# The end of an attention in a four-layer transformer kernel: transposes on TensorE against a rearranging transfer and three VectorE steps

## The chip, the cores and the metric

One core of one Trainium2 chip runs the whole program in one launch. The metric is the device time of an execution in microseconds (us), lower is better; the time before is the median of three executions, and one more execution was profiled. Engine names are those of the profile: PE (TensorE), PEld (TensorE's weight load), DVE (VectorE), ACT (ScalarE), POOL (GpSimd), SP (SyncE, which here only issues transfers).

## What is computed

Sixteen sequences of 256 tokens with 256 features pass four layers. There are seven attentions for each sequence (numbered 0 to 6; 0, 2 and 4 are self-attentions, 0 and 2 causal, 4 with a mask; 1, 3, 5 and 6 attend to a context of 77 tokens), two feed-forward blocks and one mixture of 8 experts. Every attention has 16 heads of 16 features:

```
q = q_in @ wq + bq;  k = kv_in @ wk + bk;  v = kv_in @ wv + bv
p = softmax(q @ k.T / sqrt(16))            # per head
o = concat_heads(p @ v)                    # tokens x 256
x = x + o @ wo + bo                        # then a layer norm
```

With a softmax whose rows sum to one, adding bv to v and adding it to o is the same, and the kernel adds it to o.

## The kernel before

The program has three phases. Phase a takes each sequence through attentions 0 to 3 and the first feed-forward block and routes its tokens to experts; phase b runs the experts, 39 groups of 256 tokens; phase c does attentions 4 to 6 and the second feed-forward block. In a and c a sequence is a lane: several sequences are under way at once (LANES: 6 in a, 7 in c), each at another place of its chain, so that one's transfers and small steps lie under another's matrix work.

The order on each engine is written out ahead by a planner (`Plan.run`). Each piece of work is a step with an engine, an assumed duration `us`, for transfers an assumed landing time `lag` (times a factor, 1.35), the steps it comes `after`, and the buffers that it takes and gives back. The planner places steps greedily, the earliest start first, and among equals by urgency; a table `AHEAD` shifts the urgency of each kind of step at each attention. What comes out is a fixed order for each engine: an engine that waits for one step waits with everything behind it. The names of the kinds are the ones used below:

- `proj`, `high`, `rest`, `middle`, `low`, `copy`: queries and keys are projected (PE, L684), cut into three bf16 parts by ACT, DVE and POOL, and stacked by SP's transfers (L1347) into `qs` and `ks`.
- `qm`, `max`: scores with queries on partitions (PE, L706, with the mask matmuls L839 and L843), and their maxima (DVE, L1085), one PSUM bank at a time, of eight.
- `shift_high` to `shift_low`, `turn_shift`, `turned_shift`, `shift_in`: the maxima go as three bf16 parts (DVE, L1091 to L1104) through a transpose (PE, L714) and ACT into `qs` by a transfer (L1350).
- `km`, `exp`: scores with keys on partitions (PE, L726), and their exponentials (ACT, L936) into `prob`.
- `pv`: values times probabilities (PE, L742), with 32 stationary columns for each head: 16 values, a column of ones for the sum, and 15 columns that belong to the next head and aren't used.
- the end: `raw` (ACT, L947) copies a bank of 128 partitions (4 heads of 32 rows) by 512 columns (2 groups of heads, 256 tokens) from PSUM; `turn_raw` (PE, L752) makes 4 transposes for each half of the tokens, 8 in all; `recip` and `weigh` (DVE, L1110 and L1116) divide each half by its 16 sums, with tokens on partitions; `turn_normed` (PE, L761) transposes back, 4 of them; `heads` (ACT, L953) adds bv as a per-partition bias while copying from PSUM.
- `out`, `add`: the output projection (PE, L778) and the addition to x (DVE, L1122). L778 is also the second matrix of the feed-forward blocks and experts, L794 the first.
- norms: `stats`, `moments`, `apply` (DVE, L1053, L1060, L1067) with two small POOL steps between them, then `turn` (PE, L675).
- phase c gets its tokens by `enter` and four `gather`s for each sequence (POOL, L1303) into `pair_y`.

In the names of tiles `a_`, `b_` and `c_` stand for the phase.

## Time and profile before

| | |
|---|---|
| median of three executions | 3278.52 us |
| lowest and highest | 3277.52 and 3300.14 us |
| the profiled execution, its own time | 3263.0 us |
| its span, first to last instruction | 3261.2 us |
| mean granted clock of TensorE | 0.960 of full |
| attentions | 112 (16 sequences x 7): 64 in phase a, 48 in c |

The span leaves 1.8 us around it. The profiled execution was 15.5 us (0.5%) under the median, so a sum made in the trace is put on the median's scale by the factor 3278.52 / 3263.0 = 1.0048.

### The profile page before, as it was taken

To read this page: it belongs to the slowest core of one execution; us is meant where nothing else is said; L and a number is where in the kernel's file an instruction comes from. 1 tells how busy PE (TensorE), PEld (TensorE's weight loads), DVE (VectorE), ACT (ScalarE), POOL (GpSimd) and SP (SyncE) were. 2 spreads that over 40 slices of the span, in tenths; PEclk is the share of its full clock that TensorE was granted. 3 is DMA by queue.
4 is the path that set the end of the run, shared out by engine and by line. 5 is a ranking of instruction groups with operands and counts; after the bars stand their busy time and mean duration, and the time that the engine had idled before them with its cause. 6 is when DMAs were issued, how large, how long until landed. Compare 5 with 4: busy or idle time off the path is not lost. (4 is left out here: it accounts for less than half of the span.)

```text
span 3261.2 us, 61820 instructions
## 1 busy us (share of the span) xinstructions
PE 3031.6 (93%) x23913; PEld 2467.9 (76%) x24016; DVE 1574.7 (48%) x4057; ACT 1548.4 (47%) x3403; POOL 871.0 (27%) x991
## 2 busy tenths in 40 slices
PE   7899999999999999885999999889999999999996
PEld 5788877788887788663888888656777777777774
DVE  4544556655466656353101011166555666666552
ACT  4555555564655656352222222145556555665552
POOL 3112224232223423222000000152233343433241
PEclk8999999899999999995999999989999999999997
DMA  9635446535445743832666666374425564556231
GB/s 169 95 54 67 63 54 99 81 65 70 78 59 73 108 59 70 186 49 96 235 220 222 198 204 202 101 118 64 60 49 75 77 85 62 78 76 78 39 57 26
DMA packets 394607, 319.34 MB, mean 98 GB/s; under 512 B 151711, under 2 KB 378271, under 8 KB 394303
## 3 DMA queue, kind: packets, MB, share of 16 engines
q1 hardware_dynamic: 371062, 276.77, 47.1%
q0 software_dynamic: 8272, 23.73, 3.1%
q10 hardware_dynamic: 14981, 14.89, 1.6%
q8 instruction: 190, 3.11, 0.5%
q14 instruction: 102, 0.84, 0.1%
HBM read 134.33 MB, written 37.22 MB: 53 GB/s over the span
## 5 line engine op out<-in xcount | busy, mean ns | idle before, releaser
L1085 DVE TENSOR_REDUCE a_maxima<-a_bank 128x2 f32<-128x512 f32 (+3 forms) x576 | 340.1, 646 | 136.8 <-PE a_bank L706 136.2
L936 ACT ACTIVATE a_prob<-a_bank 128x512 f32<-128x512 f32 (+1 forms) x640 | 338.1, 599 | 121.3 <-PE a_bank L726 114.9
L936 ACT ACTIVATE c_prob<-c_bank 128x512 f32<-128x512 f32 (+1 forms) x512 | 263.7, 599 | 142.5 <-PE c_bank L726 140.8
L972 ACT ACTIVATE b_group_hidden<-b_bank,b_b 128x256 f32<-128x256 f32 x312 | 131.0, 471 | 421.3 <-PE b_bank L794 421.3
L1085 DVE TENSOR_REDUCE c_maxima<-c_bank 128x2 f32<-128x512 f32 (+2 forms) x448 | 266.3, 638 | 93.1 <-PE c_bank L706 91.8
L839 PE MATMUL a_bank<-a_causal_b,keep_identb 128*128 128x256 bf16 (+1 forms) x768 | 246.2, 321 | 43.0 <-DMA a_qs<-a_shift 25.5
L794 PE MATMUL b_bank<-b_group_xt,b_w 128*128 128x256 f32 x1248 | 284.0, 381 | 0.8 <-DVE b_group_xt L1126 0.8
L778 PE MATMUL b_bank<-b_w,b_group_hidden 128*128 128x256 f32 x1248 | 275.8, 379 | 0.9 <-ACT b_group_hidden L972 0.9
L778 PEld LDWEIGHTS b_bank<-b_w,b_group_hidden 128*128 128x128 f32 x1248 | 237.0, 190 | 33.5 <-ACT b_group_hidden L972 1.3
L794 PEld LDWEIGHTS b_bank<-b_group_xt,b_w 128*128 128x128 f32 x1248 | 235.5, 191 | 31.9 <-DVE b_group_xt L1126 1.2
L1131 DVE TENSOR_TENSOR b_group_y<-b_bank,b_b 128x512 f32<-128x512 f32 x39 | 27.0, 691 | 364.4 <-PE b_bank L778 364.4
L1122 DVE TENSOR_TENSOR a_tok<-a_bank,a_tok 128x512 f32<-128x512 f32 x80 | 55.2, 690 | 190.5 <-PE a_bank L778 190.2
L706 PE MATMUL a_bank<-a_ks,a_qs 96*128 96x128 bf16 x1536 | 145.4, 223 | 0.0
L726 PE MATMUL a_bank<-a_qs,a_ks 99*128 99x128 bf16 x1536 | 145.0, 223 | 0.0
L706 PEld LDWEIGHTS a_bank<-a_ks,a_qs 96*128 96x128 bf16 x1536 | 122.9, 100 | 25.0 <-issue 3.3
L726 PEld LDWEIGHTS a_bank<-a_qs,a_ks 99*128 99x128 bf16 x1536 | 122.7, 100 | 22.5 <-issue 1.4
L778 PE MATMUL a_bank<-a_at_o,a_heads 128*128 128x256 f32 x512 | 132.0, 403 | 6.3 <-ACT a_heads L953 6.0
L684 PE MATMUL a_bank<-a_xt,a_at_q 128*128 128x256 f32 x512 | 126.7, 391 | 5.0 <-ACT a_xt L909 2.9
L1284 POOL TENSOR_TENSOR c_tok<-c_tok,weights_row_L_xattn_ln_g 128x512 f32<-128x512 f32 x64 | 81.4, 1273 | 185.6 <-PE c_bank L675 185.6
L1292 POOL TENSOR_TENSOR a_parts_q<-a_rest,a_parts_q 128x512 bf16<-128x512 f32 x64 | 74.2, 1159 | 206.6 <-ACT a_parts_q L925 206.5
L947 ACT ACTIVATE a_raw<-a_bank 128x512 f32<-128x512 f32 x128 | 76.5, 598 | 108.1 <-PE a_bank L742 107.9
L794 PE MATMUL c_bank<-c_xt,c_weights_f 128*128 128x256 f32 x512 | 122.4, 383 | 0.8 <-ACT c_xt L909 0.7
(239 smaller groups left out, 6496.2 us busy)
## 6 DMA issues: line engine op xcount, KB each, us to landing
b_w<-in_L_xattn_e_w SPq DMA_DIRECT2D x78, 1024.0 KB, 7.1
a_qs<-a_parts_q SPq DMA_DIRECT2D x384, 128.0 KB, 4.4
c_qs<-c_parts_q SPq DMA_DIRECT2D x288, 128.0 KB, 4.3
a_ks<-a_parts_k SPq DMA_DIRECT2D x192, 128.0 KB
c_ks<-c_parts_k SPq DMA_DIRECT2D x96, 128.0 KB
b_group_x<-sorted_in SPq DMA_DIRECT2D x39, 256.0 KB, 6.6
sorted_out<-b_group_y ACTq DMA_DIRECT2D x39, 256.0 KB, 4.8
sorted_in<-a_zeros SPq DMA_DIRECT2D x8, 1024.0 KB, 10.4
```

Source lines behind the costliest of these rows:

```text
L684: ins = pe.matmul(bank[:, 0, m * n:(m + 1) * n], weight[:, kt, m * P:(m + 1) * P], xt[:, kt, 0:n], start=(kt == 0), stop=(kt == KT - 1))
L706: ins = pe.matmul(bank[:, 0, to:to + m], qs[0:STACK, h, q * P:(q + 1) * P], ks[0:STACK, h, kt * P:kt * P + m], start=(at in CROSS), stop=( ...
L726: ins = pe.matmul(bank[0:kn, 0, to:to + m], ks[0:STACK + NPART, h, kt * P:kt * P + kn], qs[0:STACK + NPART, h, q0:q0 + m], start=(at in CR ...
L778: ins = pe.matmul(bank[:, 0, q * D:(q + 1) * D], heads[:, kt, q * P:(q + 1) * P], weight[:, kt, :], start=(kt == 0), stop=(kt == kts - 1))
L794: ins = pe.matmul(bank[:, 0, j * S:(j + 1) * S], weight[:, kt, f * P:(f + 1) * P], xt[:, kt, :], start=(kt == 0), stop=(kt == KT - 1))
L839: pe.matmul(blocks, k.identb, k.causal[:, keys_first, :].unsqueeze(1).broadcast_to([P, 4 // step, P]), start=True, stop=False)
L936: act.activation(prob[0:rows, first:first + cols], bank[0:rows, 0, 0:cols], ACT.Exp, scale=SCALE).then_inc(k.own(s), 1)
L947: act.activation(tile(s, "raw"), tile(s, "bank")[:, 0, :], ACT.Copy).then_inc(k.own(s), 1)
L972: ins = act.activation(hidden[:, f, :], bank[:, 0, j * S:(j + 1) * S], ACT.Gelu, bias=b1[:, f:f + 1])
L1085: v.tensor_reduce(maxima[:, q:q + qn, h:h + n].rearrange("p q h -> p h q"), bank[:, 0, 0:cols].rearrange("p (j q n) -> p j q n", j=n, q=qn ...
L1284: pool.tensor_tensor(x, x, over(k.gains[at][0]), ALU.mult).then_inc(k.own(s), 1)
L1292: pool.tensor_tensor(parts[:, 2, :, 0:n], rest[:, :, 0:n], parts[:, 1, :, 0:n], ALU.subtract).then_inc(k.own(s), 1)
```

## The change

It replaces the end of every attention.

- The values are interleaved with ones: the stationary block of a head is now 16 pairs (value, 1), so row 2d of a head's 32 rows is the output of feature d, and row 2d + 1 the sum. `pv` has the same shapes.
- `align` and `align_last`, two SP transfers for each attention, take `raw` (128 partitions x 512) to `aligned`, 64 partitions each: even rows to slot 0 and odd rows to slot 1 of the destination partition. Values and their sums then lie beside each other, with features on partitions and tokens along the row.
- DVE takes the reciprocal of the sums (128 x 512 elements), multiplies (128 x 512), and adds bv (two instructions of 128 x 256), all in place in SBUF. The output projection reads `aligned` slot 0. The rows of wo and bv are permuted ahead on the host's side of the inputs to fit.
- `turn_raw`, `turn_normed` and ACT's `heads` are gone, and their buffers with them.
- Buffers: `tok` 7 to 8, `loaded` 2 to 1 and `prob` 4 to 3 in phase a; `raw` 4 to 3; `aligned` 2 new; `pair_y` 2 to 1 in phase c. Small tiles share an allocation.
- LANES is 7 in phase a. The planner's AHEAD tables, its rate for each phase, its landing factor in phase a, and its price of a gather are other numbers.
- The load of ones at the start of phase c goes on ACT's queue. The context weights of attention 1 are a load of their own ("1c"), ahead of its q and o weights.

```
-LANES = {"a": 6, "c": 7}
+LANES = {"a": 7, "c": 7}
...
             plan.step("scalar", "raw", b, at, i, us=0.65, after=[("pv", b, at, i)], gives=["bank"], bank=pv, raw=raw)
-    raws = {f"raw{i}": ("raw", (i,) + lab) for i in range(2)}
-    normed, heads = ("normed", lab), ("heads", lab)
-    for q in range(QT):
-        bank, recip = ("bank", ("turn_raw", q) + lab), ("recip", (q,) + lab)
-        plan.step("tensor", "turn_raw", b, at, q, us=0.44, after=[("raw", b, at, 0), ("raw", b, at, 1)]
...
-        plan.step("vector", "recip", b, at, q, us=0.28, after=[("turn_raw", b, at, q)], bank=bank, recip=recip)
-        plan.step("vector", "weigh", b, at, q, us=0.45, after=[("recip", b, at, q)] + ([("weigh", b, at, 0)] if q else []),
...
-    plan.step("tensor", "turn_normed", b, at, us=0.44, after=[("weigh", b, at, 0), ("weigh", b, at, 1)], takes=["bank", "heads"],
...
-    plan.step("scalar", "heads", b, at, us=0.87, after=[("turn_normed", b, at)], gives=["bank"],
...
+            plan.step("sync", "align_last" if i else "align", b, at, us=0.65, lag=3.5, after=[("raw", b, at, i)], behind=[("align", b, at)] if i else [],
+                      gives=["raw"], landing="aligned", raw=raw, aligned=aligned)
+    plan.step("vector", "recip", b, at, us=0.6, after=[("align", b, at), ("align_last", b, at)], aligned=aligned)
+    plan.step("vector", "weigh", b, at, us=0.6, after=[("recip", b, at)], aligned=aligned)
+    plan.step("vector", "heads", b, at, us=0.6, after=[("weigh", b, at)], aligned=aligned)
+    return aligned
...
-               "projs": 0.8, ("projs", 0): -0.4, ("projs", 1): -0.2, "pvs": -1.0, ("pvs", 0): -0.1, "scores": 0.1,
+               ("projs", 0): -0.4, ("projs", 1): -1.8, ("projs", 3): -0.4, ("projs", "l0_ff"): -0.6, "pvs": -1.0,
...
-    plan.step("sync", "load", -1, "c", "ones", us=2.0, lag=2.0, takes=["w"], landing="w", transfers=len(loads["c", "ones"]),
+    plan.step("scalar", "load", -1, "c", "ones", us=2.0, lag=2.0, takes=["w"], landing="w", transfers=len(loads["c", "ones"]),
...
-        plan.step("gpsimd", "gather", b, "c", j, us=0.95, lag=4.0, behind=[("gather", b, "c", j - 1)] if j else [("enter", b, "c")],
+        plan.step("gpsimd", "gather", b, "c", j, us=1.25, lag=4.0, behind=[("gather", b, "c", j - 1)] if j else [("enter", b, "c")],
...
-                                        values[0:kn, kt, (4 * g + j) * (HD + 1):(4 * g + j) * (HD + 1) + 32],
+                                        values[0:kn, kt, 4 * g + j, :, :].rearrange("p d k -> p (d k)"),
...
         elif s.kind == "recip":
...
-            v.reciprocal(tile(s, "recip"), per_head[:, :, HD]).then_inc(k.own(s), 1)
+            sums = tile(s, "aligned")[:, 1]
+            until.wait_ge(*done("align", b, at))
+            until.wait_ge(*done("align_last", b, at))
+            v.reciprocal(sums, sums).then_inc(k.own(s), 1)
         elif s.kind == "weigh":
...
+            v.tensor_tensor(aligned[:, 0], aligned[:, 0], aligned[:, 1], ALU.mult).then_inc(k.own(s), 1)
+        elif s.kind == "heads":
+            heads, bias = tile(s, "aligned")[:, 0], k.biases[at][2]
+            until.wait_ge(*done("weigh", b, at))
+            for kt in range(KT):
+                ins = v.tensor_scalar(heads[:, kt, :], heads[:, kt, :], bias[:, kt:kt + 1], None, ALU.add)
+            ins.then_inc(k.own(s), 1)
...
+        elif s.kind in ("align", "align_last"):
+            i, half = int(s.kind == "align_last"), P // 2
+            until.wait_ge(*done("raw", b, at, i))
+            if i == 0:
+                until.wait_ge(*freed(s, "aligned"))
+            sp.dma_start(tile(s, "aligned")[i * half:(i + 1) * half], tile(s, "raw")).then_inc(k.own(s), 16)
...
-    pool("tok", 7 if name == "a" else 8, [P, QT, D])
-    pool("loaded", 2, [P, QT, D])
+    pool("tok", 8, [P, QT, D])
+    pool("loaded", 1 if name == "a" else 2, [P, QT, D])
...
-    pool("values", 2, [P, QT, H + 1, HD + 1])
+    pool("values", 2, [P, QT, H, HD, 2])
...
-    pool("prob", 4 if name == "a" else 3, [P, prob_width])
-    pool("raw", 4, [P, 2 * S])
-    pool("normed", 1, [P, QT, D])
-    pool("recip", 4, [P, H])
-    pool("heads", 1, [P, KT, S])
+    pool("prob", 3, [P, prob_width])
+    pool("raw", 3, [P, 2 * S])
+    pool("aligned", 2, [P, 2, KT, S])
...
-        plan.run("a", 20.0, ahead_of("a"), 1.35)
+        plan.run("a", 20.0, ahead_of("a"), 1.2)
...
-        lane_pool("pair_y", 2, [P, 2 * QT, D])
+        lane_pool("pair_y", 1, [P, 2 * QT, D])
...
-        plan.run("c", 28.0, ahead_of("c"), 1.35)
+        plan.run("c", 32.2, ahead_of("c"), 1.35)
```

The planner's new numbers move nearly every row, so the order is shown at two places. First DVE in the middle of phase c of the kernel before, in a run of maxima (L1085): the end of an attention is the four rows L1110 and L1116, one pair for each half of the tokens.

```order
L1075 SCALAR_TENSOR_TENSOR c_rest<-c_bank,keep_columns,c_parts_k 128x77 x2
L1085 TENSOR_REDUCE c_maxima<-c_bank 128x2
L1110 RECIPROCAL c_recip<-c_bank 128x16
L1116 TENSOR_TENSOR c_normed<-c_bank,c_recip 128x256
L1110 RECIPROCAL c_recip<-c_bank 128x16
L1116 TENSOR_TENSOR c_normed<-c_bank,c_recip 128x256
L1085 TENSOR_REDUCE c_maxima<-c_bank 128x2 x5
L1122 TENSOR_TENSOR c_tok<-c_bank,c_tok 128x512
```

The same engine and phase in the changed kernel, in which the line numbers are others (L1058 are the maxima, L1083 the reciprocal, L1087 `weigh`, L1092 `heads`, L1048 `rest`, L1064 to L1077 the four `shift` steps). This is sequence 8, attention 4.

```order
L1083 RECIPROCAL c_aligned<-c_aligned 128x512
L1058 TENSOR_REDUCE c_maxima<-c_bank 128x2
L1087 TENSOR_TENSOR c_aligned<-c_aligned 128x512
L1058 TENSOR_REDUCE c_maxima<-c_bank 128x3x2 x2
L1048 SCALAR_TENSOR_TENSOR c_rest<-c_bank,keep_columns,c_parts_k 128x77 x2
L1058 TENSOR_REDUCE c_maxima<-c_bank 128x2
L1092 TENSOR_SCALAR c_aligned<-c_aligned,keep_columns 128x256 x2
L1058 TENSOR_REDUCE c_maxima<-c_bank 128x2
L1064 TENSOR_SCALAR c_least_parts<-c_maxima 128x2x16
L1068 SCALAR_TENSOR_TENSOR c_least_rest<-c_maxima,c_least_parts 128x32
L1073 CAST c_least_parts<-c_least_rest 128x2x16
L1077 TENSOR_TENSOR c_least_parts<-c_least_rest,c_least_parts 128x2x16
```

The reciprocal has 512 elements a row where it had 16 twice, and other lanes' maxima and `shift` steps stand right behind it on the same engine.

Second PE. Phase c of the kernel before: the return transpose (L761) and, some rows on, the output projection of the same attention (L778); its 8 `turn_raw` transposes (L752) stand 7 rows above the first row shown.

```order
L761 MATMUL c_bank<-keep_identity,c_normed 128x128 x4
L843 MATMUL c_bank<-c_weights_mask_q,keep_identb 128x512
L706 MATMUL c_bank<-c_ks,c_qs 128x256 x2
L742 MATMUL c_bank<-c_prob,c_ctx_values 32x256 x8
L843 MATMUL c_bank<-c_weights_mask_q,keep_identb 128x512
L706 MATMUL c_bank<-c_ks,c_qs 128x256 x2
L726 MATMUL c_bank<-c_qs,c_ctx_ks 77x256 x8
L778 MATMUL c_bank<-c_weights_at_o,c_heads 128x256 x4
```

PE of the changed kernel at the end of the same attention as above (sequence 8, attention 4). L823 and L703 are a mask and a score matmul of `qm`, L774 a feed-forward matrix, L739 `pv`, L690 a value projection, L758 the output projection, L711 `turn_shift`, which waits for the last row of DVE's piece.

```order
L774 MATMUL c_bank<-c_xt,c_weights_f 128x256 x4
L739 MATMUL c_bank<-c_prob,c_ctx_values 32x256 x8
L823 MATMUL c_bank<-c_weights_mask_q,keep_identb 128x512
L703 MATMUL c_bank<-c_ks,c_qs 128x256 x2
L690 MATMUL c_bank<-c_weights_at_v,c_ctx_t 77x256 x2
L758 MATMUL c_bank<-c_weights_at_o,c_aligned 128x256 x4
L711 MATMUL c_bank<-keep_identb,c_least_parts 96x128 x2
```

No transposes stand between `pv` and the output projection now; the projection waits for DVE's last `heads` instruction, and `turn_shift` behind it for the DVE rows that stand behind that.

## Rows read from the trace of the kernel before

**Rows 1.** The page, part 1: busy us, share of the span and instructions.

```profile
PE 3031.6 (93%) x23913; PEld 2467.9 (76%) x24016; DVE 1574.7 (48%) x4057; ACT 1548.4 (47%) x3403; POOL 871.0 (27%) x991
```

**Rows 2.** Windows: length, then busy us of PE, PEld, DVE, ACT, POOL; clock, DMA share, GB/s.

```profile
2561.32:2694.33 133.01, 130.17 (x1045) 102.76 (x1061) 86.42 (x205) 76.15 (x168) 53.52 (x60) 1.00 0.58 75
0.00:1539.00 1539.00, 1397.27 (x12885) 1143.86 (x12885) 832.85 (x2324) 803.92 (x1746) 424.97 (x484) 0.94 0.52 82
1539.00:2101.00 562.00, 558.25 (x2652) 490.64 (x2652) 58.01 (x89) 131.00 (x312) 17.27 (x27) 1.00 0.62 201
2101.00:3261.00 1160.00, 1076.12 (x8377) 833.42 (x8480) 683.83 (x1644) 613.52 (x1345) 428.76 (x480) 0.97 0.48 69
```

**Rows 3.** The chain that ended last, in order of time: start, us, what.

```profile
2561.32 6.91 PE c_bank L778 x32
...
2694.33 6.91 PE c_bank L778 x32
```

**Rows 4.** Timeline of PE, phase a: start, us, line, operation, count.

```profile
707.48 1.04 PE L752 MATMUL a_bank<-keep_identity,a_raw 128*128 128x128 f32 x8
...
715.26 0.60 PE L761 MATMUL a_bank<-keep_identity,a_normed 128*128 128x128 f32 x4
```

**Rows 5.** Groups by form: count | busy us, mean ns | idle before, releaser.

```profile
L752 PE MATMUL a_bank<-keep_identity,a_raw 128*128 128x128 f32 x512 | 72.4, 281 | 3.0 <-ACT a_raw L947 2.2 <-DVE a_normed L1116 0.8
L752 PE MATMUL c_bank<-keep_identity,c_raw 128*128 128x128 f32 x384 | 54.9, 279 | 0.9 <-ACT c_raw L947 0.9
...
L953 ACT ACTIVATE a_heads<-a_bank,keep_columns 128x256 f32<-128x256 f32 x128 | 53.7, 473 | 64.8 <-PE a_bank L761 64.3
...
L761 PE MATMUL a_bank<-keep_identity,a_normed 128*128 128x128 f32 x256 | 41.4, 286 | 6.0 <-DVE a_normed L1116 6.0
```

**Rows 6.** Groups by form, DVE.

```profile
L1085 DVE TENSOR_REDUCE c_maxima<-c_bank 128x2 f32<-128x512 f32 x256 | 164.6, 684 | 38.1 <-PE c_bank L706 37.9
...
L1122 DVE TENSOR_TENSOR a_tok<-a_bank,a_tok 128x512 f32<-128x512 f32 x80 | 55.2, 690 | 190.5 <-PE a_bank L778 190.2
...
L1116 DVE TENSOR_TENSOR a_normed<-a_bank,a_recip 128x256 f32<-128x256 f32 x128 | 54.3, 424 | 4.2
```

**Rows 7.** Single lines, DVE: duration ns as min/median/max, first and last start, forms.

```profile
L1110 DVE RECIPROCAL a_recip<-a_bank x128: 223/256/259, 69.7 to 1501.5; 128x16 f32<-128x16 f32 x128
L1171 DVE RECIPROCAL a_route_rsum<-a_route_sum x16: 131/166/167, 476.3 to 1516.8; 128x2 f32<-128x2 f32 x16
L1158 DVE TENSOR_TENSOR a_route_logit<-a_bank,a_router_b x16: 140/170/176, 475.1 to 1515.7; 128x16 f32<-128x16 f32 x16
L1186 DVE TENSOR_TENSOR a_route_gap<-a_route_top x16: 148/154/156, 478.4 to 1517.9; 128x2 f32<-128x2 f32 x16
L1067 DVE TENSOR_SCALAR c_tok<-c_tok,c_moments,c_rstd x160: 381/407/1431, 2116.3 to 3252.6; 128x256 f32<-128x256 f32 x160
```

**Rows 8.** Transfers: a queue's packets, MB, share; issues with count, KB, us to landing.

```profile
q1 hardware_dynamic: 371062, 276.77, 47.1%
...
c_qs<-c_parts_q SPq DMA_DIRECT2D x288, 128.0 KB, 4.3
...
x_moe_in<-a_tok SPq DMA_DIRECT2D x16, 256.0 KB, 2.2
...
c_pair_y<-sorted_out,keep_rows POOLq DMA_INDIRECT x64, 5.4
```

**Rows 9.** Groups by form: DVE's `apply` in phase c, and PE's `turn` behind it.

```profile
L1067 DVE TENSOR_SCALAR c_tok<-c_tok,c_moments,c_rstd 128x256 f32<-128x256 f32 x160 | 92.5, 619 | 33.5 <-POOL c_rstd L1277 33.4
...
L675 PE MATMUL c_bank<-keep_identity,c_tok 128*128 128x128 f32 x256 | 39.7, 279 | 12.0 <-DVE c_tok L1067 12.0
```

**Rows 10.** Timeline of PE at the drain of phase a.

```profile
1419.72 1.09 PE L752 MATMUL a_bank<-keep_identity,a_raw 128*128 128x128 f32 x8 [0.72 <-ACT a_raw L947]
1423.48 3.62 PE L778 MATMUL a_bank<-a_at_o,a_heads 128*128 128x256 f32 x8 [0.82 <-ACT a_heads L953]
```

**Rows 11.** Timeline of SP: three transfer issues back to back.

```profile
726.81 1.89 SPq L1347 DMA_DIRECT2D a_ks<-a_parts_k  x3
```

127 lines of the change are left out of this document (54 added, 73 removed).

## The prediction, made before the changed kernel ran

> **What bounds the kernel now.** I read the page first: PE is busy for 93% of the span, DVE for 48% and ACT for 47% [rows 1]. Next the windows: PE is busy for 1397 of 1539 us in phase a, 558 of 562 in b and 1076 of 1160 in c [rows 2]. Third the chain: in the middle of phase c the same feed-forward matrix comes back at 2561.32 and at 2694.33 us, two sequences later, so a sequence takes 66.5 us there [rows 3], and PE is busy for 130.2 of those 133.0 us [rows 2]. Matmuls are pipelined and a busy PE isn't PE at its peak, but instructions that leave such a stream give their slots back. So PE bounds a and c, and phase b isn't touched. In the same 133 us DVE is busy for 86.4, or 43.2 us for a sequence, and ACT for 38.1 [rows 2]. Their waits cost nothing now. The question is what the change puts on DVE.
>
> **What PE loses.** Each attention had 8 transposes `turn_raw` and 4 `turn_normed`. Eight in a row take 1.04 us and four take 0.60 [rows 4]. The difference of 0.44 us for four gives 0.110 us each; the mean of 281 ns in the groups [rows 5] is the latency of one, not its slot. 112 attentions x 12 x 0.110 = 147.8 us: 84.5 in phase a, 63.4 in c. On a PE that is busy without a break all of it comes off: **-148**. `pv` keeps its count and shapes, 32 stationary columns and as many moving ones; nothing there.
>
> **What ACT loses.** 112 x 2 `heads` instructions of 0.47 us [rows 5], 106 us, all beside PE's work: 0.
>
> **What DVE gets, the disputed term.** Gone are two reciprocals of 128 x 16 (0.256 us) [rows 7] and two products of 0.424 [rows 6], 1.36 us for an attention. New are:
> - `weigh`, 128 x 512: 0.69, as the addition of that size [rows 6].
> - `heads`, two of 128 x 256: 2 x 0.41, the median of `apply`, the same operation and size [rows 7].
> - `recip`, 128 x 512, which the trace doesn't show. The lower bound is an ordinary operation of that size, 0.68 to 0.69 (a maximum, an addition) [rows 6]. For the upper I compare small ones. A tensor_tensor grows from 154 ns at 2 elements to 170 at 16, about 1 ns an element. The reciprocal starts at nearly the same place, 166 ns at 2 elements, but is at 256 at 16: 90 ns for 14 elements, 6.4 ns each [rows 7]. A fixed extra cost would show at 2 elements, and it doesn't. On a line, 512 elements take 0.166 + 510 x 0.0064 = 3.45 us. The two points differ in that one reads PSUM, but so does the 170 ns row. I take **3.45**.
>
> The Trainium skill, "VectorE: DVE Perf Modes", section "First, the fixed hardware budget", says that the reciprocal is an iterative divide on two slices with a repeat count of 8. The trace agrees that it is several times slower for each element than other operations, with 6.4 ns. Were it 8 cycles at the page's 0.96 GHz, an estimate from that page alone is 4.27 us for each, and the sum below would come out some 31 us higher.
>
> So DVE works 0.69 + 0.81 + 3.45 = 4.95 us for an attention where it worked 1.36. In the steady middle of phase c that is 43.2 - 4.1 + 14.9 = 54.0 us for a sequence, against 66.5 - 4.0 = 62.5 us that PE would take: 86% busy. DVE isn't the bound by its sum, but it is one in stretches. The order of DVE (front matter) has the reciprocal, `weigh`, `heads`, five maxima, `rest` and four `shift` steps ahead of `turn_shift`; with the durations above and the rows' for the rest that is about 10 us, and PE's work from the same point to its `turn_shift`, priced the same way, about 9.
>
> The planner put these orders together with 0.6 + 0.6 + 0.6 = 1.8 us (in the diff). DVE will take 3.15 us more than the order allows for, 112 times: 353 us. What stands behind it in DVE's queue are other lanes' maxima (which free PSUM banks for `qm`), `shift` steps (awaited by `turn_shift`) and `apply` (awaited by `turn`). PE follows a fixed order too, so a late one stops everything on PE, unless the awaited result had time in hand. How much passes on is the second unknown, between 0 and all. The nearest rows are `apply` in phase c. Its mean is 619 ns and its median 407, with some at 1431: 160 x 0.212 = 34 us of delay in pieces of up to 1 us [rows 7, 9]. PE waited 12.0 us for it [rows 9]: at most 35%, and part of that belongs to the start of the phase. Pieces of 3 us use up time in hand that pieces of 1 us don't. Against that, the planner counts 3.5 x 1.35 us for a landing in c, more than a copy's 4.3 or a 256 KB store's 2.2 [rows 8]. I take a third: 353 / 3 = **+118**, with 15% to 50% as the likely band.
>
> **The transfers.** 224 of 256 KB. An issue takes SP 0.63 us (three in 1.89) [rows 11]; that is 6 more in a phase c sequence, 4 us of SP's 62. The transfer queue used 47.1% of 16 engines for 276.8 MB [rows 8], so 0.262 MB cost 1.5 us of all engines, 8.7 us for a sequence in c, where the share is 0.58 [rows 2]: it rises to about 0.7. That is a load, not a bound: 0, if landings stay below 5 us. SP waits at `align` for `raw` with other lanes' copies behind it, but the planner orders by the same step, and ACT's delays get fewer. Where nothing covers the chain, it counts whole. At the drain of phase a, `turn_raw` to the projection took 3.76 us (1419.72 to 1423.48) [rows 10]. The new way is 0.63 + 3.3 for the landing (between 2.2 and 4.3) + 4.95 = 8.9, that is 5.1 us more, for about two attentions at the end of each phase: **+20**.
>
> **Buffers, lanes, loads.** One `pair_y` makes a sequence's gathers wait for the mix before it; they land in 5.4 us [rows 8], far less than the 62 us of a sequence, so it costs only at phase c's start, up to 8 us. The load of ones leaves SP at the same place and gives back about 2. A seventh lane in a, and the fresh tables, can win part of the 142 us that PE stands idle in that phase [rows 2], or lose as much by fewer buffers. I take 0, -30 to +30.
>
> **Sum.** 3263.0 - 148 + 118 + 20 = 3253 on the profiled execution's scale, whose span is 1.8 us shorter. That execution was 0.5% under the median, so x 1.0048: **3269 us**. By the band of what passes on (53 to 177 us) it is 3203 to 3328.
>
> **Rivals.**
> - *The reciprocal runs at the ordinary rate*, 0.69 us. For it: I extrapolate from 16 elements to 512. Against it: 166 against 256 ns. DVE then takes 2.2 us, 0.4 over the planner's figure; a third of 44 us passes, +15, and the ends cost +10: 3263 - 148 + 25 = 3140, x 1.0048 = **3155**.
> - *DVE takes PE's place*, the one on the slow side. With maxima at 0.68 us a bank [rows 6] against two score matmuls and a mask on PE, which run ahead only as far as eight banks reach, a reciprocal inside a run of maxima leaves PE with nothing to do. At 65% passed on: 3263 - 148 + 229 + 20 = 3364, **3381**. It decides from (148 - 20) / 353 = 36% upward, close to what I take, which is why its chance isn't small.
> - *The transfers are late*: landings of 8 us or more with 14% more load, and every projection waits: some 4 us for half the attentions, +220 on the fast case, about 3380 as well.
> - *It doesn't do what it says*: PE's slots aren't given back, since the chains bind. The steady 66.5 us speak against it; it would be no change.
>
> **Chances.** The reciprocal is slow in about three of four cases. Likeliest (slow, 15% to 50% passed on) 0.44; full gain 0.27; DVE in PE's place 0.24; late transfers and the rest 0.05. A measurement of this kernel tells about 1% from no change (33 us: its three executions spread over 23). The full gain is faster throughout. Of the likeliest case about 0.12 lies below 3246, 0.27 within, 0.05 above. Faster 0.38, same 0.29, slower 0.33. The range that leaves out some 2 in 10 goes from 3135, under the full gain, to 3375, which holds almost half of the slow rival.
>
> **What would show it.** Right or wrong at once: the mean of the reciprocal at 128 x 512 (3.4 or 0.7). Then the period of a sequence in the middle of phase c (62.5 us if nothing passes, 66.5 at no gain), DVE's share there (86% of 62.5), PE's idle time put down to maxima, `shift` steps and `aligned`, and the landing time of `aligned`. I am wrong if the reciprocal is at the ordinary rate, or if DVE's lateness passes on nearly whole.

## The result, and the profile after

The changed kernel takes **3699.94 us** (median of 4 runs, 3692.12 to 3701.87) against 3284.96 (3277.52 to 3300.14) for the kernel before: a ratio of **1.126**, with an interval of 1.123 to 1.128. The forecast was 3269 with a range of 3135 to 3375. The profiled execution has a span of 3697.2 us.

Page, part 1 (against [rows 1]), and the queue that carries the copies (against [rows 8]):

```profile
PE 3060.0 (83%) x22672; PEld 2407.1 (65%) x22672; DVE 1943.5 (53%) x4048; ACT 1457.3 (39%) x3179; POOL 875.6 (24%) x991
...
q1 hardware_dynamic: 403204, 335.44, 55.5%
```

Windows of the three phases (against [rows 2]):

```profile
0.00:1760.00 1760.00, 1405.22 (x12120) 1107.38 (x12121) 1055.13 (x2319) 749.59 (x1618) 427.37 (x484) 0.88 0.62 91
1760.00:2320.00 560.00, 557.25 (x2650) 489.74 (x2648) 58.09 (x89) 131.01 (x312) 17.33 (x27) 1.00 0.62 201
2320.00:3697.00 1377.00, 1097.58 (x7904) 809.98 (x7904) 830.30 (x1640) 576.72 (x1249) 430.90 (x480) 0.88 0.57 76
```

Phase b is what it was. Phase a grew by 221 us and c by 217, and in neither did PE work much longer: outside its busy time PE stood 3697.2 - 3060.0 = 637 us, before 3261.2 - 3031.6 = 230. So 408 of the 436 us between the spans are idle time of PE. The other 28 are stranger: with 1344 transposes gone, PE is busy for longer than before. (Of the kernel before, 103 matmul records are missing: 23913 against 24016 weight loads. At some 0.2 us each, the distance of such matmuls in the timeline, its busy time reads at most about 20 us too low, an estimate; the transposes alone were about 148.) The granted clock fits: 0.94 and 0.97 in a and c before [rows 2], 0.88 in both now.

The costliest groups behind the change (busy us, mean ns | idle before, releaser):

```profile
L1083 DVE RECIPROCAL a_aligned<-a_aligned 128x512 f32<-128x512 f32 x64 | 214.3, 3349 | 213.2 <-DMA a_aligned<-a_raw 213.1
...
L758 PE MATMUL a_bank<-a_at_o,a_aligned 128*128 128x256 f32 x512 | 171.8, 494 | 129.6 <-DVE a_aligned L1092 115.8
...
L758 PE MATMUL c_bank<-c_weights_at_o,c_aligned 128*128 128x256 f32 x384 | 131.5, 502 | 129.3 <-DVE c_aligned L1092 100.1
...
L1083 DVE RECIPROCAL c_aligned<-c_aligned 128x512 f32<-128x512 f32 x48 | 160.7, 3348 | 118.3 <-DMA c_aligned<-c_raw 118.3
```

The reciprocal takes 3.35 us, and ahead of it DVE stands for 213 + 118 us more, waiting for the transfer with everything that is queued behind. The output projection (L758) stands 259 us, 216 of them for DVE's bias addition on the same tile. Single lines (ns as min/median/max, first and last start) and the transfers (KB, us to landing):

```profile
L1083 DVE RECIPROCAL a_aligned<-a_aligned x64: 3319/3352/3354, 70.4 to 1718.6; 128x512 f32<-128x512 f32 x64
...
L1092 DVE TENSOR_SCALAR c_aligned<-c_aligned,keep_columns x96: 340/348/1247, 2414.4 to 3681.3; 128x256 f32<-128x256 f32 x96
```

```profile
a_aligned<-a_raw SPq DMA_DIRECT2D x128, 256.0 KB, 5.3
...
c_aligned<-c_raw SPq DMA_DIRECT2D x96, 256.0 KB, 7.8
```

One attention in the middle of phase c, on the chain that ended last (start, us, what):

```profile
2835.67 0.61 SPq L1329
2836.27 0.04 issue
2836.32 9.01 DMA c_aligned<-c_raw
...
2845.42 3.36 DVE c_aligned L1083
2848.78 0.02 issue
2848.81 0.70 DVE c_aligned L1087
...
2850.20 3.78 PE c_bank L758 x8
```

From the transfer's issue to the projection it is 14.5 us; I had put the whole chain at 8.9. Then comes the part that no sum of mine had. The same eight matmuls take 2.0 us elsewhere, 3.78 here. The timeline of PE shows both, in brackets the idle time ahead of them:

```profile
2809.22 1.99 PE L758 MATMUL c_bank<-c_weights_at_o,c_aligned 128*128 128x256 f32 x8 [2.70 <-DVE c_aligned L1092]
...
2850.20 3.78 PE L758 MATMUL c_bank<-c_weights_at_o,c_aligned 128*128 128x256 f32 x8 [6.40 <-DVE c_aligned L1092]
```

Windows over the slow eight, over the fast eight, and over the idle time ahead of the slow ones (length, busy us of PE, PEld, DVE, ACT and POOL, clock, DMA share, GB/s):

```profile
2850.20:2854.00 3.80, 3.80 (x9) 2.83 (x10) 1.74 (x5) 0.96 (x2) 1.63 (x2) 0.50 1.09 112
2809.20:2811.20 2.00, 1.98 (x9) 1.63 (x10) 0.00 (x0) 0.00 (x0) 0.00 (x0) 1.00 0.00 0
2844.00:2850.00 6.00, 0.00 (x0) 0.00 (x0) 4.51 (x4) 0.00 (x0) 0.00 (x0) 0.90 1.23 124
```

Behind 6.40 us without work the projection ran at a granted clock of 0.50, 1.2 GHz; behind 2.70 us it ran at 1.00. So a long wait costs more than its length, and a shorter one need not. The Trainium skill, "TensorE: Matmul & The Clock Gate", section "Part 1: The HAM clock gate (the "warmup" mystery)", says that a gate sets the clock by how busy PE has been of late; the trace agrees, with 0.50 behind the longer of the two waits and 1.00 behind the shorter. In the kernel before, the projection's groups were these:

```profile
L778 PE MATMUL a_bank<-a_at_o,a_heads 128*128 128x256 f32 x512 | 132.0, 403 | 6.3 <-ACT a_heads L953 6.0 <-DVE a_normed L1116 0.2
...
L778 PE MATMUL c_bank<-c_weights_at_o,c_heads 128*128 128x256 f32 x384 | 94.5, 390 | 2.3 <-ACT c_heads L953 2.1
```

With the same counts its busy time rose by 39.8 and 37.0 us, 77 in all, while matmuls of the feed-forward layers, which never wait, kept their 0.38 to 0.39 us.

Two feed-forward matrices, nine sequences apart, on PE's timeline of phase c (against [rows 3]):

```profile
2563.69 7.17 PE L758 MATMUL c_bank<-c_weights_f,c_qs 128*128 128x256 f32 x32
...
3264.99 7.17 PE L758 MATMUL c_bank<-c_weights_f,c_qs 128*128 128x256 f32 x32
```

701.3 / 9 = 77.9 us for a sequence in the mean, before 66.5. Before, the distances in the steady part were 66.5 each time; now single ones lie between 26 us (2702.29 to 2728.24) and 134 us (2815.63 to 2949.22). I had named 62.5 (nothing passes) and 66.5 (no gain).

### The profile page after: what moved, and what is told of

It reads as the page before. It is cut to its first block and busy times, and to the rows that moved or that the text cites. A ratio compares the mean times of both kernels' runs of the same rounds, so it can differ in the third digit from the quotient of the medians.

```text
span 3697.2 us, 59072 instructions
## 1 busy us (share of the span) xinstructions
PE 3060.0 (83%) x22672; PEld 2407.1 (65%) x22672; DVE 1943.5 (53%) x4048; ACT 1457.3 (39%) x3179; POOL 875.6 (24%) x991
## 3 DMA queue, kind: packets, MB, share of 16 engines
q10 hardware_dynamic: 15095, 14.95, 1.3%
## 5 line engine op out<-in xcount | busy, mean ns | idle before, releaser
L1058 DVE TENSOR_REDUCE a_maxima<-a_bank 128x2 f32<-128x512 f32 (+2 forms) x576 | 339.6, 646 | 97.9 <-PE a_bank L703 91.3
L1058 DVE TENSOR_REDUCE c_maxima<-c_bank 128x2 f32<-128x512 f32 (+2 forms) x448 | 263.8, 637 | 127.4 <-PE c_bank L703 124.9
L1083 DVE RECIPROCAL a_aligned<-a_aligned 128x512 f32<-128x512 f32 x64 | 214.3, 3349 | 213.2 <-DMA a_aligned<-a_raw 213.1
L819 PE MATMUL a_bank<-a_causal_b,keep_identb 128*128 128x256 bf16 (+1 forms) x768 | 255.2, 332 | 73.0 <-DMA a_qs<-a_shift 22.6
L774 PE MATMUL b_bank<-b_group_xt,b_w 128*128 128x256 f32 x1248 | 284.5, 381 | 0.8 <-DVE b_group_xt L1102 0.8
L758 PE MATMUL a_bank<-a_at_o,a_aligned 128*128 128x256 f32 x512 | 171.8, 494 | 129.6 <-DVE a_aligned L1092 115.8
L758 PE MATMUL b_bank<-b_w,b_group_hidden 128*128 128x256 f32 x1248 | 275.8, 379 | 0.9 <-ACT b_group_hidden L945 0.9
L758 PEld LDWEIGHTS b_bank<-b_w,b_group_hidden 128*128 128x128 f32 x1248 | 237.0, 190 | 33.5 <-ACT b_group_hidden L945 1.3
L774 PEld LDWEIGHTS b_bank<-b_group_xt,b_w 128*128 128x128 f32 x1248 | 235.7, 191 | 32.1 <-DVE b_group_xt L1102 1.2
L758 PE MATMUL c_bank<-c_weights_at_o,c_aligned 128*128 128x256 f32 x384 | 131.5, 502 | 129.3 <-DVE c_aligned L1092 100.1
L758 PEld LDWEIGHTS a_bank<-a_at_o,a_aligned 128*128 128x128 f32 x512 | 120.5, 247 | 161.3 <-DVE a_aligned L1092 139.3
L1083 DVE RECIPROCAL c_aligned<-c_aligned 128x512 f32<-128x512 f32 x48 | 160.7, 3348 | 118.3 <-DMA c_aligned<-c_raw 118.3
L758 PEld LDWEIGHTS c_bank<-c_weights_at_o,c_aligned 128*128 128x128 f32 x384 | 93.2, 254 | 157.0 <-DVE c_aligned L1092 130.6
L723 PE MATMUL a_bank<-a_qs,a_ks 99*128 99x128 bf16 x1536 | 153.4, 230 | 0.0
L703 PE MATMUL a_bank<-a_ks,a_qs 96*128 96x128 bf16 x1536 | 150.3, 229 | 0.0
L703 PEld LDWEIGHTS a_bank<-a_ks,a_qs 96*128 96x128 bf16 x1536 | 127.1, 103 | 27.8 <-issue 8.5
```

The costliest lines, as they stand in the source:

```text
L703: ins = pe.matmul(bank[:, 0, to:to + m], qs[0:STACK, h, q * P:(q + 1) * P], ks[0:STACK, h, kt * P:kt * P + m], start=(at in CROSS), stop=( ...
L723: ins = pe.matmul(bank[0:kn, 0, to:to + m], ks[0:STACK + NPART, h, kt * P:kt * P + kn], qs[0:STACK + NPART, h, q0:q0 + m], start=(at in CR ...
L758: ins = pe.matmul(bank[:, 0, q * D:(q + 1) * D], heads[:, kt, q * P:(q + 1) * P], weight[:, kt, :], start=(kt == 0), stop=(kt == kts - 1))
L774: ins = pe.matmul(bank[:, 0, j * S:(j + 1) * S], weight[:, kt, f * P:(f + 1) * P], xt[:, kt, :], start=(kt == 0), stop=(kt == KT - 1))
L819: pe.matmul(blocks, k.identb, k.causal[:, keys_first, :].unsqueeze(1).broadcast_to([P, 4 // step, P]), start=True, stop=False)
L1058: v.tensor_reduce(maxima[:, q:q + qn, h:h + n].rearrange("p q h -> p h q"), bank[:, 0, 0:cols].rearrange("p (j q n) -> p j q n", j=n, q=qn ...
```

## The experiments

Every kernel was timed beside the kernel before on the same chip, and ratios are to that; its medians were 3277, 3289, 3272 and 3286 us in the four sessions. The theories: **R**, the long reciprocal in DVE's order; **L**, the transfer, as wait or as load; **P**, the orders, lanes and smaller buffers.

### First session: what is the reciprocal's part?

**e1**, a product of the same size in the reciprocal's place:

```diff
-            v.reciprocal(sums, sums).then_inc(k.own(s), 1)
+            v.tensor_tensor(sums, sums, sums, ALU.mult).then_inc(k.own(s), 1)
```

> The changed kernel with the reciprocal of 128 x 512 replaced by a product of the same size and place (the division is left out: the output is wrong by that). DVE gives up 3.35 - 0.69 = 2.66 us for each of 112 attentions, 298 us. If the reciprocal's length is the cause (theory R), PE's lost time goes with it and the kernel is at 3155 us, the figure of my fast rival. If it is that DVE, in order, stands in front of a landing of 5.3 to 7.8 us (theory L, late landings), that wait stays: DVE's idle time ahead of this line stays near 330 us and the time stays above 3450. If the order itself is bad (theory P, the planner's prices and fewer buffers) the time is also well above 3285, but with little idle time at the aligned tile.

Measured 3527.43 us, ratio 1.078 (1.075 to 1.081). The division is left out. R explains 1.126 - 1.078, 157 us; some 60% of the loss stay. DVE still stands ahead of the cheap operation as before:

```profile
L1083 DVE TENSOR_TENSOR a_aligned<-a_aligned 128x512 f32<-128x512 f32 x64 | 49.9, 780 | 225.4 <-DMA a_aligned<-a_raw 225.4
```

**e2**, the planner told of DVE's real durations:

```diff
-    plan.step("vector", "recip", b, at, us=0.6, ...
-    plan.step("vector", "weigh", b, at, us=0.6, ...
-    plan.step("vector", "heads", b, at, us=0.6, ...
+    plan.step("vector", "recip", b, at, us=3.38, ...
+    plan.step("vector", "weigh", b, at, us=0.72, ...
+    plan.step("vector", "heads", b, at, us=0.72, ...
```

> The changed kernel with the planner told what the trace shows for DVE: 3.38 us for the reciprocal, 0.72 for the product, 0.72 for the two bias additions, instead of 0.6 each. Same instructions, another order. Theory P (a wrong price puts other lanes' work in the wrong place) expects most of the loss back: below 3450 us. Theory R in its plain form (DVE's work itself is too long for any order) expects 3600 to 3700; theory L as well, since the landing is still priced at 3.5 times the phase's factor.

Measured 3666.12 us, 1.122 (1.117 to 1.126): not to be told from the changed kernel. The wrong price, on which I had hung the whole third that passes on, isn't a cause by itself. DVE's wait for the landing stayed (211.6 us in a).

**e3**, both transfers issued by ACT behind its eviction instead of by SP:

```diff
-            plan.step("sync", "align_last" if i else "align", ...
+            plan.step("scalar", "align_last" if i else "align", ...
```

> The changed kernel with the transfer of the values and sums issued by ACT, right behind its own eviction, instead of by SP, where it stood behind other lanes' copies. SP gives up 224 issues of 0.63 us. Theory L expects the wait of DVE ahead of the reciprocal (213 + 118 us) to fall by half and the kernel by 100 us or more; theory R expects less than 50 us either way, since the reciprocal stays.

Measured 3654.53 us, 1.115 (1.111 to 1.118), about 36 us less. DVE's wait fell from 331 to 278 us (180.2 and 97.7), not by half. The transfers here also leave the copies' queue for ACT's (that queue goes from 14.95 to 73.69 MB). So SP's place in the chain and the order within the copies' queue are together a small part.

**e4**, the kernel before with DVE made slow:

```diff
+            v.reciprocal(per_head[:, :, HD + 1:32], per_head[:, :, HD + 1:32])
             v.reciprocal(tile(s, "recip"), per_head[:, :, HD]).then_inc(k.own(s), 1)
```

> The kernel before, with one more reciprocal of 128 x 240 (PSUM columns that nobody reads, in place) ahead of each of its two small ones: about 1.7 us each by 6.5 ns an element, 3.4 us for an attention, 381 us of DVE in all. No transfer, no buffer and no order is touched. Theory R expects most of what the changed kernel lost to DVE: +300 us or more, 3580 to 3700. My own prediction's share of a third would give +127, 3410. Theory L (the landing is the cause) expects no more than +100, 3385.

Measured 3560.99 us, 1.089 (1.085 to 1.092). The added work:

```profile
L1110 DVE RECIPROCAL a_bank<-a_bank 128x240 f32<-128x240 f32 x128 | 212.5, 1660 | 128.8 <-PE a_bank L752 128.2 <-issue 0.2
L1110 DVE RECIPROCAL c_bank<-c_bank 128x240 f32<-128x240 f32 x96 | 159.3, 1660 | 59.8 <-PE c_bank L752 59.8
```

372 us of instructions more on DVE cost 284: **76% passes on**. (DVE's busy time rose by less, 335 us, to 54% of the span; by that it is 85%.) The share of a third was wrong, even where nothing but DVE is touched. The time is a little under R's band.

### Second session: without the transfer

**e5** and **e6** keep the changed kernel's order on every engine, but SP issues no transfer and DVE works on a tile of ones after waiting for ACT's eviction, so the attention's result is left out; e6 has the product in the reciprocal's place too. ACT's eviction doesn't wait for a free `raw` tile in them. That hides little: in the changed kernel such waits for a transfer come to 2.9 us (`c_raw`).

```diff
+        if tile == "raw":
+            return "start", 0
...
-            until.wait_ge(*done("align", b, at))
-            until.wait_ge(*done("align_last", b, at))
+            until.wait_ge(*done("raw", b, at, 1))
+            until.wait_ge(*k.freed_late(b, at))
...
-            sp.dma_start(tile(s, "aligned")[i * half:(i + 1) * half], tile(s, "raw")).then_inc(k.own(s), 16)
+            pass
```

> The changed kernel without its transfers: SP leaves the two issues out, and DVE's reciprocal, product and bias additions run in place on a tile filled with ones, waiting for ACT's eviction instead of a landing (the attention's result doesn't reach the projection; the output is wrong by that). Every engine's order is the changed kernel's. 224 x 256 KB, their load on the transfer engines and their landing time are gone, the long reciprocal stays. Theory L expects most of the 250 us that stayed with the cheap reciprocal to go here: 3450 to 3500, and DVE's idle time ahead of the reciprocal well under 150 us (331 before). Theory P (orders, fewer buffers) expects 3600 or more.

> As e5_no_transfer, with the reciprocal replaced by a product of its size. Neither the long reciprocal nor the transfer: what is left of the change are the 148 us of transposes that PE is spared, 0.8 us more on DVE for each attention, the new tables and the smaller buffers. R and L together expect 3150 to 3250, below the kernel before. Theory P expects 3350 or more.

Measured e5 3468.17 us, 1.054 (1.052 to 1.056); e6 3341.97, 1.017 (1.014 to 1.019). With e1 they make a square:

```text
ratio to before        real reciprocal   product in its place
with transfer          1.126             1.078
without transfer       1.054             1.017
```

The transfer costs 0.061 to 0.072, **200 to 237 us**; the reciprocal 0.037 to 0.048, **121 to 157 us**. DVE's idle time ahead of the reciprocal in e5 is 31.3 us in a and 12.6 in c, as theory L said. What is left in e6 is 1.7% slower than before, though the transposes are gone: R and L together had promised 3150 to 3250.

**e7**, e2 and a longer landing for the planner:

```diff
-            plan.step("sync", "align_last" if i else "align", b, at, us=0.65, lag=3.5, ...
+            plan.step("sync", "align_last" if i else "align", b, at, us=0.65, lag=5.5, ...
```

> The changed kernel with the planner told of DVE's real durations and of a landing of 5.5 us (times 1.2 in phase a and 1.35 in c: 6.6 and 7.4) in place of 3.5 (4.2 and 4.7). DVE then gets the reciprocal later in its order. Theory L with order as its carrier (DVE stands because the order brings it to the reciprocal before the landing) expects DVE's idle time there to fall under 150 us and the kernel to 3450 to 3550. If the longer chain simply moves the wait to PE's projection, it stays within 50 us of 3666.

Measured 3635.66 us, 1.106 (1.104 to 1.109). The wait of DVE falls to a third:

```profile
L1083 DVE RECIPROCAL a_aligned<-a_aligned 128x512 f32<-128x512 f32 x64 | 214.0, 3343 | 81.8 <-DMA a_aligned<-a_raw 81.8
L1083 DVE RECIPROCAL c_aligned<-c_aligned 128x512 f32<-128x512 f32 x48 | 160.3, 3340 | 30.8 <-DMA c_aligned<-c_raw 30.6
```

219 us of DVE's idle time went, and 64 us of the kernel's. So DVE standing at the landing was mostly a symptom; the 331 us can't be read as a cost. On PE the waits for the `aligned` tile fell from 216 to 84 us, while those for copies into `qs` and `ks` rose from 88 to 145 (sums over all rows of the view of waits).

**e8**, the kernel before with the changed kernel's smaller pools:

```diff
-    pool("loaded", 2, [P, QT, D])
+    pool("loaded", 1 if name == "a" else 2, [P, QT, D])
-    pool("prob", 4 if name == "a" else 3, [P, prob_width])
-    pool("raw", 4, [P, 2 * S])
+    pool("prob", 3, [P, prob_width])
+    pool("raw", 3, [P, 2 * S])
-        lane_pool("pair_y", 2, [P, 2 * QT, D])
+        lane_pool("pair_y", 1, [P, 2 * QT, D])
```

> The kernel before with the changed kernel's smaller pools: one entry tile and three probability tiles in phase a, three eviction tiles, one tile for gathered rows in c. I predicted 0 (-30 to +30) for these. If the buffers are a cause of the remaining 250 us, this is at 3350 or more; otherwise 3265 to 3310.

Measured 3351.13 us, 1.019 (1.017 to 1.020): **+62 us** for pools that I had put at 0 with 30 to either side. The planner knows the pools and makes its order by them, so this is the price of fewer buffers together with the order that comes of them.

### Third session: what do the transposes give back?

**e9**, the kernel before with 1 transpose for 4 in each turn step (9 of 12 gone; what follows reads the first 128 columns over again):

```diff
-            for g in range(H // 4):
+            for g in range(1):
                 ins = pe.transpose(bank[:, 0, g * P:(g + 1) * P],
...
-            for q in range(QT):
-                for kt in range(KT):
+            for q in range(1):
+                for kt in range(1):
                     ins = pe.transpose(bank[:, 0, kt * S + q * P:kt * S + (q + 1) * P], ...
```

> The kernel before with 1 transpose instead of 4 in each of its three turn steps, 9 of 12 gone for each attention; the reciprocal, the product and ACT's eviction keep their sizes and read the first 128 columns over again (the attention's result is wrong by that). Waits, DVE's and ACT's work, buffers and orders are untouched. It measures the term that I put at -148 for 12: 112 x 9 x 0.110 = 111 us less, 3170 to 3180, if PE gives back every slot. If the chains around PE hold it (theory S, the slots go into waits), less than half: 3230 or more.

Measured 3222.71 us, 0.985 (0.980 to 0.989): 50 us for nine (35 to 66), where I had 111. Its page:

```profile
PE 2954.6 (92%) x22915; PEld 2370.7 (74%) x23008; DVE 1576.5 (49%) x4057; ACT 1540.2 (48%) x3403; POOL 870.8 (27%) x991
```

PE's busy time fell by 77 us [rows 1], and its idle time rose from 230 to 265. Of the 111 us, 34 went in slower matmuls, with the granted clock down from 0.960 to 0.952, and 36 in waits. Neither theory's number was met; it lies nearer to S.

**e10**, e6 with more buffers:

```diff
-    pool("prob", 3, [P, prob_width])
-    pool("raw", 3, [P, 2 * S])
-    pool("aligned", 2, [P, 2, KT, S])
+    pool("prob", 4 if name == "a" else 3, [P, prob_width])
+    pool("raw", 4, [P, 2 * S], BF16)
+    pool("aligned", 2, [P, 1, KT, S])
-        lane_pool("pair_y", 1, [P, 2 * QT, D])
+        lane_pool("pair_y", 2, [P, 2 * QT, D])
```

> As e6_no_transfer_cheap (3342 us), with most of the buffers of the kernel before: four probability tiles in phase a, four eviction tiles (in bf16, to fit), two tiles for gathered rows in c; one entry tile in a stays. The first DVE operation is a difference on the same half tile, of the same size. e8 put the smaller pools at +62 us on the kernel before; if that is what is left here, this run is at 3280 or less. If the 148 us of transposes then also show, 3200 or less. Theory P (orders and seven lanes are worse) keeps it above 3300.

Measured 3288.11 us, 1.005 (1.002 to 1.007), 0.012 or 40 us under e6. So the buffers cost the new scheme about two thirds of what they cost the old. Not all are back: the entry tile in a stays one, and `raw` is in bf16 and isn't waited for here, so its fourth tile acts only through the planner's order. With them it is within half a per cent of the kernel before, on the slow side.

**e11**, e7 with the reciprocal as exp(-ln(sum)) on ACT:

```diff
-            v.reciprocal(sums, sums).then_inc(k.own(s), 1)
+            act.activation(sums, sums, ACT.Ln).then_inc(k.own(s), 1)
...
+            act.activation(sums, sums, ACT.Exp, scale=-1.0).then_inc(k.own(s), 1)
```

> e7 (true prices, landing of 5.5: 3636 us) with the reciprocal computed by ACT as exp(-ln(sum)), two activations of 128 x 512 at 0.60 us, while DVE keeps the product and the bias additions. ACT is busy for 40%, so 134 us more there should lie beside PE. The long reciprocal on DVE cost 157 us with the transfers in place (e1), so theory R expects 3460 to 3520. If the build loads an activation table at every switch between the two functions, ACT gets over 1 us for each and the time is above 3636.

Measured 3632.32 us, 1.110 (1.104 to 1.115), level with e7. DVE gave up its 374 us of reciprocals, but ACT got 141 us of activations and 284 us of table loads:

```profile
L933 ACT ACT_TABLE_LOAD x112 | 143.7, 1283 | 101.8 <-DMA a_aligned<-a_raw 51.4 <-DMA c_aligned<-c_raw 48.9
L937 ACT ACT_TABLE_LOAD x109 | 139.8, 1283 | 1.9
```

So it doesn't test R: one long operation in an ordered queue was exchanged for another.

**e12**, the edits of e8 and e9 in one kernel.

> e9 and e8 together: the kernel before with 9 of 12 transposes gone and the smaller buffers. If the two are independent, it is at 3285 + 62 - (3285 - e9). If fewer buffers let PE run less far ahead, the freed slots turn into waits and the gain of e9 shrinks here: 3300 or more (theory S).

Measured 3288.73 us, 1.005 (1.003 to 1.007). Against e8 the nine transposes give 0.014, 47 us, as they gave 50 alone: the two terms add.

### Fourth session: is the transfer a wait or a load?

**e13**, the bytes without the wait: the transfers go to a spare tile, and DVE waits as in e6. **e14**, the wait without the bytes: 64 rows of 32 elements in each transfer, and DVE waits for the landing as in e1. Both have a cheap operation for the reciprocal and leave the attention's result out.

```diff
 e13
-            sp.dma_start(tile(s, "aligned")[i * half:(i + 1) * half], tile(s, "raw")).then_inc(k.own(s), 16)
+            sp.dma_start(k.tiles["spare"][0][i * half:(i + 1) * half], tile(s, "raw")).then_inc(k.own(s), 16)
 e14
-            sp.dma_start(tile(s, "aligned")[i * half:(i + 1) * half], tile(s, "raw")).then_inc(k.own(s), 16)
+            sp.dma_start(tile(s, "aligned")[i * half:(i + 1) * half, 1, 0, 0:32], tile(s, "raw")[0:half, 0:32]).then_inc(k.own(s), 16)
```

> The changed kernel with a cheap first DVE operation (a difference in place of the reciprocal), as e1 (3527 us), but the two transfers of 256 KB go to a spare tile that nobody reads, and DVE waits only for ACT's eviction. SP's issues and waits and all the bytes stay; the result of the attention is left out. If load is the cause, it stays at 3480 or more; if latency is, it comes down to e6's 3342 plus at most 50.

> The other half: DVE waits for the landing as in e1, but each transfer carries 64 rows of 32 elements (8 KB in place of 256); the values and sums don't reach the product (the result of the attention is left out). If load is the cause, 3342 to 3390; if latency is, 3450 or more, with DVE still standing 150 us or more ahead of its first operation.

Measured e13 3455.84 us, 1.052 (1.049 to 1.055); e14 3377.43, 1.026 (1.023 to 1.030). From e6's 1.017, the load with SP's issues costs 0.035 (**116 us**), the wait for a short transfer with the same issues 0.010 (**32 us**), both in full 0.061 (200). Taken off in the other order, e1 less e14, the bytes cost 0.051 (168 us). So load is the larger part, 116 to 168 of 200 us. SP's issues and its waits for `raw` are in e13 too, but e14 has the same and costs 32 in all. The 0.016 over the sum of the two is presumably the wait made longer by the load; no run shows that by itself. The wait alone I had overrated: DVE still stood 190 us ahead of its first operation in e14, of which at most 32 reached the time.

```profile
L1083 DVE TENSOR_TENSOR a_aligned<-a_aligned 128x512 f32<-128x512 f32 x64 | 48.3, 755 | 137.6 <-DMA a_aligned<-a_raw 137.6
...
L1083 DVE TENSOR_TENSOR c_aligned<-c_aligned 128x512 f32<-128x512 f32 x48 | 35.8, 745 | 51.9 <-DMA c_aligned<-c_raw 51.9
```

Two of PE's waits for copies in e6 and then e13 (us in total, times, longest):

```profile
PE c_bank L728 <- DMA c_qs<-c_shift: 13.1, 9, 3.2
PE c_bank L708 <- DMA c_qs<-c_parts_q: 11.7, 4, 8.1
```

```profile
PE c_bank L724 <- DMA c_qs<-c_shift: 23.6, 10, 7.7
PE c_bank L704 <- DMA c_qs<-c_parts_q: 17.4, 3, 11.2
```

Over all rows of that view PE waits for copies into `qs` and `ks` for 75 us in e6, 72 in e14 and 134 in e13. So 256 KB transfers that nobody waits for make PE stand 59 us longer for the copies that the scores need; of the 121 us between the spans of e6 and e13, 72 are idle time of PE and 49 busy time, at a lower clock (0.936 to 0.920).

The landings where they are shown are less clear. `a_qs<-a_parts_q` takes 4.4 us before, 4.9 in e10 without the transfers and 6.4 in e1 with them, but `c_qs<-c_parts_q` 4.3 before [rows 8] and 5.2 in both e10 and e1. Nor is it shown that the order within the queue delays the copies: in e3 the transfers had another queue, PE still waited 90 us for copies (88 in the changed kernel), and the time fell by 36 us only.

**e15** and **e16**, six lanes instead of seven:

```diff
 e15
-LANES = {"a": 6, "c": 7}
+LANES = {"a": 6, "c": 6}
 e16
-LANES = {"a": 7, "c": 7}
+LANES = {"a": 6, "c": 6}
```

> The kernel before with six instead of seven sequences in flight in phase c. If the number in flight bounds the period (latency divided by lanes), phase c's steady part takes a sixth more, 100 us or more in all; if PE's work bounds it, less than 30 us. I argued the latter.

> The changed kernel with six lanes in both phases in place of seven. If its longer chain is bound by the number in flight (latency), it loses more than the kernel before does for a lane, 150 us or more over two phases; if DVE or the load is the bound, less than 60 us. The same run says what the seventh lane of phase a was worth.

Measured e15 3348.08 us, 1.018 (1.016 to 1.020); e16 3730.06, 1.135 (1.132 to 1.138), 0.009 over the changed kernel. A lane in c was worth 58 us to the kernel before, more than PE alone as the bound allows and less than lanes as the bound would cost. Two lanes were worth only about 31 us to the changed kernel: the number in flight isn't what binds it, and the seventh lane in a can't have paid for the buffers that made room for it.

## Why the prediction was wrong

All profiled executions side by side (idle is the span less PE's busy time):

```text
kernel                        span    PE busy  PE idle  clock
before                        3261.2  3031.6   229.6    0.960
e9, few transposes            3219.9  2954.6   265.3    0.952
e6, no transfer, cheap        3329.8  2962.4   367.4    0.936
e14, wait without load        3382.0  2979.7   402.3    0.932
e13, load without wait        3450.7  3011.8   438.9    0.920
e5, no transfer               3468.2  3011.9   456.3    0.923
e1, cheap                     3518.0  3019.1   498.9    0.913
after                         3697.2  3060.0   637.2    0.898
```

Step by step, as the prediction put them:
- **PE's -148.** The mechanism was right, the size wrong. Nine twelfths gave 50 us (e9) and 47 (e12), so twelve give about 65. I took every slot off the time because PE was busy for 130.2 of 133.0 us in one steady stretch; over phases a and c PE waits for part of what it is spared and works slower for another part. That the chains of steps hold it there is my reading; no run shows the chain.
- **ACT 0.** Right in its premise: ACT's busy time fell by 91 us. What that alone is worth no run shows.
- **The reciprocal's length.** Right: 3.35 us measured, 3.45 taken from the line through 2 and 16 elements. The estimate of 4.27 us worked out from the Trainium skill, "VectorE: DVE Perf Modes", section "First, the fixed hardware budget", is too much. `heads` took 2 x 0.35 (median), not 2 x 0.41, and DVE's busy time rose by 369 us, not by 402.
- **What passes on, a third, +118.** The term came near by luck. The reciprocal alone costs 121 us (e5 against e6) where 269 us of DVE time differ, 45%; with the transfer there 157 of 267, 59%; in the kernel before 284 of 372, 76% (e4). The waits for `apply` were a poor row to scale from, since they came in pieces of up to 1 us. And the carrier was not the planner's wrong price (e2) but more work on an in-order engine, ahead of other lanes' work. That the length of one block of 3.35 us matters is not shown: e4's came in blocks of 1.66 us and passed on more.
- **The transfers, 0.** This is the step that failed. They cost 200 us with a cheap reciprocal and 237 with the real one. I named the condition myself, "0, if landings stay below 5 us", and then read the rise of the transfer engines' share to 0.7 as "a load, not a bound" (by my own numbers it is 0.76 at the 62.5 us that I forecast). Landings came at 5.3 and 7.8 us, and the share in phase c was 0.57 (0.58 in the steady part), below the 0.7 that I foresaw, since the phase had grown with the bytes: the share didn't warn. What counts is that the bytes make the copies that PE needs come later (e13) and, with the smaller part, that the transfer is itself in the chain (e14). My rival "the transfers are late" had the size, +220, and a chance within 0.05; but it counted only the projection's wait, which by itself is the smaller part, so its size was partly luck. No row of the kernel before showed an SBUF to SBUF transfer of 256 KB; I took the middle of a copy of 128 KB at 4.3 us and a store of 256 KB at 2.2. The copy's figure alone, for half the bytes, argued for more than 4.3, and the 2.2 was the shortest of the frequent 256 KB transfers in that trace. Others stood beside it:

```profile
b_group_x<-sorted_in SPq DMA_DIRECT2D x39, 256.0 KB, 6.6
sorted_out<-b_group_y ACTq DMA_DIRECT2D x39, 256.0 KB, 4.8
...
c_loaded<-x_moe_in SPq DMA_DIRECT2D x16, 256.0 KB, 5.3
```

- **Buffers and lanes, 0 (-30 to +30).** Wrong: +62 (e8) and about 40 in the new scheme (e10). The extra lane is worth little.
- **Not in the sum: the clock.** Long waits slow the work behind them. From e6 downward, where the matmuls are the same, PE's busy time rises with its idle time in the table. The traces of e14, e13 and the changed kernel hold every matmul record: from e14 to the changed kernel idle time rises by 235 us and busy time by 80. (In e6, e5 and e1 74 records are missing, some 15 us of busy time by the same estimate.)
- **What I said would make me wrong.** The reciprocal at the ordinary rate, or DVE's lateness passing on nearly whole. Neither came; the largest miss lay in a term that I had put at 0.
- **Rivals as alternatives.** I gave late transfers and DVE in PE's place each a time of about 3380, with one chance for each. They are separate causes, and both came. With the measured sizes in my own sum, 3269 + 83 for the transposes + 39 for the reciprocal (157 less 118) + 200 for the transfer + 62 for the buffers is 3653, most of the way to 3700. My range allowed for one of them at a time.

Adding the measured terms to the kernel before in ratios: e6, in which transposes, buffers, the rest of DVE's work and the new tables lie together, +0.017; reciprocal without transfer +0.037; transfer with it +0.072; 1.126. Within e6, -65 us of transposes and +62 of buffers leave about 57 us for DVE's other new work (its busy time is 102 us over the kernel before) and the new tables. These two weren't taken apart, nor was the split of the loads.

Of the signs named ahead, the reciprocal's mean (3.35 us), the period of 77.9 us and the landings tell the cases apart. DVE's share in the steady part was 63% (362.9 of 575 us from 2560 on), not the 86% that I had worked out for a period of 62.5; the 54.0 us of DVE work that I forecast for a sequence would be 69% of 77.9. An engine busy for 63% delayed PE all the same.

No version of the new scheme beats the kernel before. The best that compute the whole result are e7 and e11, 11% slower; e10, which leaves out the transfer and the division, only comes level. The scheme saves PE's 65 us and pays 120 for the reciprocal or 200 for the transfer, each alone more than that.

## What to carry to other kernels

A chain of PE work that is exchanged for a transfer and DVE work pays with four things that its slots don't show: the landing, the copies that it delays, what stands behind the added work in an ordered queue, and the clock of the matmuls after a long wait. Price a new transfer by the wait it puts into the chain and by the other copies in flight that engines wait for, not by the share of the transfer engines; and add independent rivals instead of giving each its own chance. When PE is busy for 98% in one steady stretch, a test with part of its work left out says how much of a saving arrives: here less than half.

## What the hardware showed that I had not expected

- In these runs the reciprocal is close to linear in size: 1.660 us for 128 x 240 and 3.352 for 128 x 512 in f32, 6.2 ns for each more element; at 16 elements 0.256 [rows 7].
- A DVE bias addition of 128 x 256 in place took 0.348 us (median), in `apply`, which takes two per-partition operands, 0.407 [rows 7].
- Eight f32 matmuls of 128 x 256 took 2.0 us at a granted clock of 1.00 and 3.78 at 0.50, behind 6.40 us without work; behind 2.70 us without work they took 1.99.
- 224 transfers of 256 KB that nobody waited for cost 116 us, at a share of the copies' queue of 0.60 (e13).
- Exchanging Ln and Exp on ACT brought 221 table loads of 1.283 us, one at nearly every switch.
